# A graph network's first unweighted aggregate: one-hots scaled by a shared constant and made two groups ahead

## The reference

```
h = relu(layernorm(x));  x = x + GAT(h, src, dst)
h = relu(layernorm(x));  x = x + SAGE2(h, src, dst)

def sage_layer(h, edge_src, edge_dst, deg_inv, W_self, W_neigh, b):
    msg  = h[edge_src]
    agg  = segment_sum(msg, edge_dst, num_segments=3125)
    mean = agg * deg_inv[:, None]
    return h @ W_self + mean @ W_neigh + b
SAGE2 = sage_layer(relu(sage_layer(h, ..., W_self0, W_neigh0, b0)), ..., W_self1, W_neigh1, b1)
```

## Time and profile before

| | us |
|---|---|
| median of 3 runs | 4068.97 |
| lowest and highest | 4061.72, 4071.57 |
| the profiled execution | 4053.89 |
| its span | 4052.2 |

### The profile page before, as it was taken

The page is one execution under the profiler, slowest core; times in us unless marked ns, Lnnn a source line. Parts: engine busy times, 40 slices in busy tenths (PEclk is TensorE's granted clock), DMA queues, the critical chain, the costliest instruction groups (busy, mean ns, idle before and its releaser), DMA issues. The chain is left out here.

```text
span 4052.2 us, 74821 instructions
## 1 busy us (share of the span) xinstructions
PE 3058.3 (75%) x20638; PEld 1746.6 (43%) x20638; DVE 2648.9 (65%) x4534; ACT 1150.8 (28%) x2637; POOL 1657.4 (41%) x1788
## 2 busy tenths in 40 slices
PE   0567878388888882007999999699668999997899
PEld 0334544277777772003444444244324444442444
DVE  5646878688888887866555555555466555656443
ACT  3542343377777673310000000033200000000211
POOL 4002222366666662114555555400145555555000
PEclk9978999699999996558999999899889999999999
DMA  1456895388888885776999999622479999997333
GB/s 67 148 179 231 292 335 188 110 275 267 265 274 272 260 274 179 234 239 224 314 299 300 313 307 296 220 91 91 139 225 315 307 313 309 324 320 260 118 91 85
DMA packets 289524, 947.22 MB, mean 234 GB/s; under 512 B 57746, under 2 KB 58746, under 8 KB 289440
## 3 DMA queue, kind: packets, MB, share of 16 engines
q0 software_dynamic: 224912, 726.88, 53.8%
q1 hardware_dynamic: 64528, 219.29, 17.5%
HBM read 905.65 MB, written 130.59 MB: 256 GB/s over the span
## 5 line engine op out<-in xcount | busy, mean ns | idle before, releaser
L1434 POOL DMA_INDIRECT agg_got<-h_rows,agg_idx_now x896 | 898.0, 1002 | 654.3 <-issue 371.0
L1571 PE MATMUL agg_sum_ps<-agg_got,agg_hot 128*128 128x512 f16 x3584 | 878.1, 388 | 205.3 <-DVE agg_hot L1464 172.3
L1492 DVE TENSOR_TENSOR sum_acc<-agg_sum_ps,sum_acc 125x1024 f32 x448 | 548.7, 1225 | 434.4 <-PE agg_sum_ps L1571 322.9
L1555 PE MATMUL gagg_sum_ps<-gagg_got,gagg_hot_hi 128*128 128x256 f16 x3584 | 603.9, 274 | 198.6 <-DVE sums_acc L1492 129.3
L1571 PEld LDWEIGHTS agg_sum_ps<-agg_got,agg_hot 128*128 128x128 bf16 x3584 | 343.3, 99 | 664.0 <-DVE agg_hot L1464 216.9
L1530 ACT ACTIVATE gagg_hot_hi<-gagg_hot,gat_high_e 128x128 f16<-128x128 f16 x1792 | 547.7, 388 | 277.5 <-DVE gagg_hot L1459 229.2
L1434 POOL DMA_INDIRECT gagg_got<-xs_rows,gagg_idx_now x448 | 500.8, 1118 | 266.3 <-PE gagg_extra_ps L1560 120.5
L925 PE MATMUL agg_out_ps<-agg_w,agg_a_t 128*128 128x512 f16 x2400 | 577.3, 384 | 0.0
L818 PE MATMUL neigh_out_ps<-neigh_w,neigh_a_t 128*128 128x512 f16 x2400 | 529.3, 381 | 5.0 <-DMA neigh_w<-split_w 5.0
L1555 PE MATMUL gagg_sum_ps<-gagg_got,gagg_hot_lo 128*128 128x256 f16 x1792 | 490.5, 274 | 0.5 <-issue 0.4
L905 ACT ACTIVATE agg_a_t<-agg_turn_ps 128x2048 f16<-128x2048 f16 x50 | 93.8, 1877 | 1376.7 <-PE agg_turn_ps L913 1343.9
(11 more groups left out here) (257 smaller groups left out, 2952.4 us busy)
## 6 DMA issues: line engine op xcount, KB each, us to landing
edg_piece<-slot_rows POOLq DMA_DIRECT2D x56, 512.0 KB
agg_a<-h_rows SPq DMA_DIRECT2D x50, 448.4 KB
part_rows<-agg_rows SPq DMA_DIRECT2D x50, 448.0 KB
neigh_rows<-part_rows SPq DMA_DIRECT2D x50, 448.0 KB
edg_w_buf<-in_L_gnn_W_self_dram SPq DMA_DIRECT2D x32, 512.0 KB
edg_w_buf<-in_L_gnn_W_neigh_dram SPq DMA_DIRECT2D x32, 512.0 KB
split_w<-edg_w_out SPq DMA_DIRECT2D x32, 512.0 KB, 7.8
agg_got<-h_rows,agg_idx_now POOLq DMA_INDIRECT x896
```

The costliest lines, as they stand in the source:

```text
L1434: g.indirect_dma_start(out=got[:, k, :], out_offset=None, in_=rows_in[:, :], in_offset=bass.IndirectOffsetOnAxis(ap=idx_now[:, s, k:k + 1] ...
L1492: v.tensor_tensor(acc[:, tl, :], sum_ps[n % 2][0:TN, :].rearrange("p (a d) -> p a d", a=1), acc[:, tl, :], ALU.add).then_inc(added, 1)
L1555: t.matmul(sum_ps[n % 2][:, h * C:(h + 1) * C], hot_k[:, u % HOTS, h, :], got[:, u % R, part * D + h * C:part * D + (h + 1) * C], start=(u ...
L1571: last = t.matmul(sum_ps[n % 2][:, q * HALF:(q + 1) * HALF], hot[:, u % HOTS, :], got[:, u % R, cols], start=(u == steps[0] and part == 0) ...
```

## The change

`aggregate` gets an argument `even`. Where it is given, the one-hot is made without reading the gathered rows and without the wait for them: it is scaled by the constant `even`, and AHEAD is 2. Only `agg0` is given it, as 1/UP. PE's list, POOL's list and the waits on them stay as they are.

```
-        def aggregate(tag, rows_in, acc, acc_x=None, product=None):
+        def aggregate(tag, rows_in, acc, acc_x=None, product=None, even=None):
...
                             if weighted:
                                 v.tensor_scalar(hot[:, u % HOTS, :], iota_tn[:, :], rel[:, ds(s, 1)], None,
                                                 ALU.is_equal).then_inc(hot_ready, 1)
+                            elif even is not None:
+                                v.tensor_scalar(hot[:, u % HOTS, :], iota_tn[:, :], rel[:, ds(s, 1)], even,
+                                                ALU.is_equal, ALU.mult).then_inc(hot_ready, 1)
                             else:
...
-                    AHEAD = 2 if weighted else 1
+                    AHEAD = 2 if weighted or even is not None else 1
...
-            aggregate("agg0", h_rows, acc, product=(SELF0, b0, None, part0_rows))
+            aggregate("agg0", h_rows, acc, product=(SELF0, b0, None, part0_rows), even=1.0 / UP)
```

## The result

The changed kernel took 4033.84 us (median of 4 runs, 4029.95 to 4038.94), the kernel before 4069.18 us in the same set (4 runs, 4061.72 to 4071.57). The ratio is 0.9917, interval 0.9902 to 0.9933: 35 us faster, where 25 were forecast. The profiled execution of the changed kernel, 4038.94 us with a span of 4037.3 us, is the highest of its runs, and that of before, 4053.89 us, lies 15 us under its median. The two traces are therefore only 15 us apart. By its interval the ratio stands for 27 to 40 us.

A forecast was written before the change was run, and what follows sets the result against it. PE was taken to bound agg0's rounds with a product, held up once a round by DVE's order. Heads 19, start 1.5, rounds without a product 1.5 and clock 3 make 25 us: 4069 - 25 = 4044 us, range 4022 to 4067.

The forecast's parts named there:

- the likeliest case: The forecast itself: agg0's head stall shrinks and moves to group 2; gain 13 to 36 us, chance 0.59.
- the heads: 24 round heads in agg0: chain wins 1.0 us each, taken as 0.8 for late rows, 19 us in all.
- the start: Start of agg0: group 1 and a product piece run during the clearing of acc; 1.5 us, ends 0 and 3.9.
- end of agg0: Last three rounds, without a product: POOL is the limit, DVE no longer stops for rows; 1.5 us, ends 0 and 4.4.
- clock in agg0's rounds: Three half-clock stretches of PE behind pauses, 1.7 us each; one expected to stay, so 3 us gained.
- That addition stands behind the same jump: agg0's head: group 0's addition stays at about 2289.95, one-hots bring 0.1 us; group 2 stalls 1.0 us.
- Mostly off that path: DVE's waits for rows in agg0, 32.5 us, end well ahead of PE's need because one-hots are made early.
- Nothing outside agg0 moves: All other stages, agg1 among them, were to keep their times.
- One (the transfers): agg0's DMA gives no more than about 304 to 308 GB/s; gain 0 to 12 us, about 4063 us; chance 0.26.
- Two (the whole stall goes): agg0's heads lose the whole 2.0 us because group 2 does not wait for the addition; 4013 us; chance 0.06.
- Three (the clock slower): New pauses halve PE's clock at every head of agg0; 19 us slower, 4088 us; chance 0.07.
- four (gathers of 1118 ns): POOL's gathers in agg0 take 1118 ns against 993, costing 6 us in the last three rounds; 4050 us; chance 0.02.

The follow-up runs named there:

- the second run of the changed kernel: The changed kernel measured once more, unedited: 4013.29 us, ratio 0.9916 to the kernel before in its set.
- the last set: Final runs, including both kernels unedited on one chip: the kernel before 3959.91 us (ratio 1.0009), the changed kernel 3927.82 us (0.9932).
- number first: Changed kernel with the tile's number of group 1 loaded at the head of agg0's round, ahead of the one-hots: 3942.19 us, ratio 0.9955.
- the order alone: Changed kernel, but agg0's one-hots, still two groups ahead, read their row's factor and wait for the row: 4079.96 us, ratio 1.0069.
- the taking-out first: Changed kernel with agg0's product taken out on DVE ahead of the wait for group 7 and its addition: 3894.09 us, ratio 0.9832.
- the taking-out first on the kernel before: Kernel before with agg0's product taken out ahead of the wait for group 7 and its addition: 3918.23 us, ratio 0.9899.

## Why the prediction was right, and where it was not

The forecast was 4044 us; 4033.84 came out, inside its range and at the lower edge of the likeliest case (4033 to 4056), which is by its mechanism the one that happened: the stall moved from group 1 to group 2 and shrank. Its sum, however, came near with the wrong parts: the heads gave 9 to 12 of their 19 us, and the start and agg1, put at 1.5 us together, gave 10 to 13. That these errors offset each other was luck. Here it is term by term, in us gained, from three pairs of traces: the first (before and after), before against the second run of the changed kernel, and the pair of the last set. The measured rows of the heads and the clock are the 23 distances; the first round stands with the start, the 24th head with the end.

| term | forecast | first | second | third |
|---|---|---|---|---|
| 24 heads, without half-clock stretches | 19 | 12.3 | 9.8 | 9.4 |
| start | 1.5 | 6.4 | 4.7 | 7.3 |
| end of agg0 | 1.5 | -1.8 | 1.8 | 1.6 |
| clock in agg0's rounds, at 1.7 a stretch | 3 | 1.7 | 5.1 | 0 |
| agg1 | 0 | 3.9 | 8.5 | 5.7 |
| sum | 25 | 22.5 | 29.9 | 24.0 |

What is left to the 35, 34 and 27 us of the runs lies in stages that the change does not touch, and, in the first pair, in the 20 us by which its two profiled executions stand off their medians on opposite sides.

**The head, 19.** The step that failed is the size in "That addition stands behind the same jump (1.57 us), behind two one-hots (now of group 2) and behind a gap of 1.05 us, so it stays at about 2289.95", and the 0.1 us that shorter one-hots were to bring. That the addition stays is right: over the 25 heads it starts 4.90 us after the end of group 7's addition, before and after the change. But the earlier trace rows show a quick head, with 4.48 us from one to the other; the one in the timeline of the changed kernel has 5.02. The gap ahead of the addition, read as 1.05 us, is 1.47 us on average in the same trace (0.81 to 1.96) and 1.76 us in the changed one (0.84 to 2.53). It took up what shorter one-hots gave, since the load that stands in it ends 2.90 us behind the jump in both (number first). So the mean stall that is left is 1.55 to 1.66 us and not 1.0, and the gain is about 0.4 to 0.5 us a head, not 0.8 to 1.0. A gap that nobody waited for was read from one row and taken to be typical. The forecast's other half held: no matmul waits for a one-hot at the head, the idle time is put down to the addition, and no second stall follows.

**"Mostly off that path".** The waits of DVE for rows were priced at nothing. The constant alone, with the order unchanged, gained 13 to 27 us, and the order alone lost 22 to 34. So the order that I took for the source of nearly all of the gain is worth about 14 us, 7 to 9 of them in the rounds, and only because the constant frees it from the rows. What the waits cost in the rounds was near to nothing as forecast (2 to 3 us); at the start it was 5 us. That they end ahead of PE's need in the round that I looked at was true; what they did to other rounds, to the start and to DVE's additions I did not add up.

**The start, 1.5.** "The clearing itself starts at nearly the same time" failed. In the old kernel the first one-hot waited for its rows and the clearing stood behind it. From the load of the weights to the clearing it was 25.1 us and is now 20.4 (24.6 and 20.6 in the first pair):

```profile
1733.31 0.35 DVE L1464 TENSOR_SCALAR agg_hot<-all_iota_tn,all_rel,agg_got 128x128 bf16<-128x128 f32 x1 [8.12 <-DMA agg_got<-h_rows,agg_idx_now]
...
1740.19 21.39 DVE L1502 MEMSET sum_acc<- 125x25600 f32 x1 [5.28 <-issue]
```
```profile
1725.04 0.87 DVE L1462 TENSOR_SCALAR agg_hot<-all_iota_tn,all_rel 128x128 bf16<-128x128 f32 x4 [4.21 <-DMA agg_bias_sb<-in_L_gnn_b_dram]
...
1731.19 21.39 DVE L1505 MEMSET sum_acc<- 125x25600 f32 x1 [5.28 <-issue]
```

The first two rows are the last set's kernel before, the other two its changed kernel. These 4 to 4.7 us were read as "a wait for rows less" and not priced. What is left of the measured term, 1.0 to 2.7 us, fits the 1.5 that was forecast. The end of agg0 came out at -1.8 to 1.8 us, so that its 1.5 is neither borne out nor refuted.

**The clock, 3.** The stretches in agg0's rounds went from 3 to 2, from 3 to 0 and from 1 to 1. The forecast of one that stays is as good as the scatter allows. By the rule of the Trainium skill, "TensorE: Matmul & The Clock Gate", "The HAM clock gate", all would go; one pair of the three did so, and the changed kernel's three traces have 2, 0 and 1.

**"Nothing outside agg0 moves".** agg1, whose code is the same, is 3.9 to 8.5 us shorter. The rows of windows over its rounds in the last set, before and then changed (window, us, busy time of PE, PEld, DVE, ACT and POOL, granted clock, DMA share, GB/s):

```profile
2845.00:3557.00 712.00, 626.11 (x3079) 285.51 (x3078) 427.04 (x649) 45.05 (x24) 400.82 (x433) 0.96 0.93 304
```
```profile
2822.00:3529.00 707.00, 619.18 (x3081) 283.13 (x3080) 429.69 (x649) 45.05 (x24) 400.85 (x433) 0.97 0.93 306
```

Nearly the same number of matmuls takes 6.9 us less at a slightly higher clock. agg1 has 7 to 9 half-clock stretches in all five traces of kernels whose agg0 one-hots read the rows, and 1 to 5 in the nine others. What agg0 leaves behind that decides this was not found.

**The rivals.** One (the transfers) falls: half of them bring only some 7 us, and the taking-out first ran at 331 GB/s, above the 314 of the earlier trace rows. Two (the whole stall goes) did not happen; it takes one more move on DVE. Three (the clock slower) did not happen. In four (gathers of 1118 ns) the gathers beside the new one-hots took 993 ns, so their length in the weighted aggregate does not come from such one-hots.

**Left open:** the cause in agg1; what keeps the second load of the tile's number until 2.9 us behind the jump; and whether executions under the profiler favour the kernel before (15, 5 and 5 us under its medians and 17 for the order alone, which waits for rows as well; but 3 above for the taking-out first on the kernel before).

## What to carry to other kernels

When an instruction is moved earlier in an in-order queue, price what then stands in front of it: the same order was worth some 14 us with operands that are always ready and cost 28 us with operands that come by DMA. Read a gap on which a stall is to land from all of its occurrences and not from one: this one ran from 0.81 to 1.96 us. And at a loop's end put last an instruction that runs on while the jump and the loads pass, not one whose result the engine waits for: with that move and the 1.28 us that it took off the path, the kernel before became 40 us faster, and with the change 67 us.

## What the runs showed of the hardware

- In agg0 the second load of a number into a register behind DVE's loop jump took 1.1 to 1.4 us on average in a trace (0.4 to 2.1 in a head), where nearly all others took 0.3 us. It ended 2.9 us behind the jump on average, whether it started 1.1, 1.6 or 1.8 us behind it. With both loads ahead of the one-hots DVE's gap there was 3.6 us on average.
- Gathers and the rest of agg0's traffic ran at 331 GB/s on one core beside a PE that was idle for 7.0 us in 585 us of rounds; 304 to 310 GB/s in the slower rounds was demand, not supply.
- A one-hot with a constant in place of a second operand per partition took 285 to 297 ns on average in agg0 (nine traces), against 351 to 358 ns (five traces).
